# Splitting minus the score maxima before the transpose: bf16 products, a dense copy, and one 512-column addition per head

## What is computed

```python
scores = jnp.einsum('bhqd,bhkd->bhqk', q, k) / np.sqrt(D_HEAD)      # window, cells, masked
scores = jnp.where(local[None, None, :, :], scores, -jnp.inf)       # windowed attention only
attn = jax.nn.softmax(scores, axis=-1)
ctx = jnp.einsum('bhqk,bhkd->bhqd', attn, v)
```

## Time and profile before

| | |
|---|---|
| median of 3 runs | 3567.08 us (3566.13 to 3568.82) |
| the profiled execution | 3568.07 us, of which the span is 3566.3 us |
| PE busy | 3242.3 us, 91% of the span |
| DVE, ACT, POOL busy | 65%, 48%, 29% |
| granted TensorE clock, mean | 0.964 of full speed |
| stores of the 16 results | first at 510.4 us, last at 3563.7 us |

### The profile page before, as it was taken

The page is one execution under the profiler, slowest core; times in us unless marked ns, Lnnn a source line. Parts: engine busy times, 40 slices in busy tenths (PEclk is TensorE's granted clock), DMA queues, the critical chain, the costliest instruction groups (busy, mean ns, idle before and its releaser), DMA issues.

```text
span 3566.3 us, 77500 instructions
## 1 busy us (share of the span) xinstructions
PE 3242.3 (91%) x31372; PEld 2395.2 (67%) x31372; DVE 2329.9 (65%) x4137; ACT 1695.1 (48%) x3472; POOL 1019.1 (29%) x795
## 2 busy tenths in 40 slices
PE   7899999998999999899999999999899999999876
PEld 6777767676766667676666766667676666766644
DVE  6675658667676766767577675766767676464533
ACT  1244454544545455444635445354454545554532
POOL 7872006042331413333041332304233141000000
PEclk8999999999999999999999999999999999999986
DMA  6210011010101101010100101101010110100000
GB/s 207 89 45 31 19 29 39 29 40 19 46 19 40 31 23 46 16 41 26 37 28 25 43 19 37 31 29 39 19 46 19 40 31 16 37 14 10 13 7 4
DMA packets 123276, 122.88 MB, mean 34 GB/s; under 512 B 9776, under 2 KB 122672, under 8 KB 122800
## 3 DMA queue, kind: packets, MB, share of 16 engines
q1 hardware_dynamic: 122928, 117.91, 10.9%
HBM read 113.69 MB, written 4.19 MB: 33 GB/s over the span
## 4 chain that ended last, share of the span: by engine, by line
PE 60%; DVE 15%; ACT 9%; issue 8%; POOL 7%; DMA 1%; SPq 0%; DVEq 0%; POOLq 0%; ACTq 0%
PE banks L747 16%; PE banks L739 11%; PE banks L892 7%; PE banks L917 6%; DVE nmx L1251 5%; PE banks L945 5%; POOL work L1641 3%; ACT work L1482 3%; PE banks L732 2%; PE banks L754 2%; PE banks L855 2%; PE banks L903 2%; POOL work L1631 2%; PE banks L952 1%; PE banks L921 1%
## 5 line engine op out<-in xcount | busy, mean ns | idle before, releaser
L747 PE MATMUL banks<-work,weights 128*128 128x256 f32 x3584 | 868.3, 390 | 56.4 <-DVE work L1275 51.5
L1251 DVE TENSOR_REDUCE nmx<-banks 128x4 f32<-128x1024 f32 (+3 forms) x684 | 725.4, 1099 | 250.5 <-PE banks L892 248.7
L747 PEld LDWEIGHTS banks<-work,weights 128*128 128x128 f32 x3584 | 678.3, 194 | 189.0 <-DVE work L1275 53.9
L1482 ACT ACTIVATE work<-banks 128x1024 f32<-128x1024 f32 (+3 forms) x679 | 595.1, 937 | 288.7 <-PE banks L921 288.7
L739 PE MATMUL banks<-weights,work 128*128 128x256 f32 x2688 | 653.7, 389 | 20.7 <-ACT work L1482 4.4
L739 PEld LDWEIGHTS banks<-weights,work 128*128 128x128 f32 x2688 | 499.3, 193 | 124.9 <-issue 39.7
L1641 POOL TENSOR_TENSOR work<-work 128x512 f32<-128x512 f32 x256 | 407.3, 1615 | 366.4 <-DVE work L1221 216.9
L892 PE MATMUL banks<-work 32*128 32x256 f32 (+1 forms) x5120 | 357.5, 394 | 60.5 <-DVE nmx L1251 27.2
L917 PE MATMUL banks<-work 32*128 32x256 f32 (+1 forms) x5120 | 391.4, 394 | 18.0 <-DVE nmx L1251 6.8
L1631 POOL TENSOR_TENSOR work<-work 128x512 f32<-128x512 f32 x256 | 346.6, 1375 | 148.7 <-DVE work L1217 134.7
L1269 DVE TENSOR_TENSOR added<-work 128x1024 f32<-128x1024 f32 x192 | 281.3, 1469 | 129.3 <-ACT work L1482 118.7
(11 more groups left out here) (156 smaller groups left out, 3525.2 us busy)
## 6 DMA issues: line engine op xcount, KB each, us to landing
weights<-in_w_all SPq DMA_DIRECT2D x322, 256.0 KB, 2.8
work<-in_w_setup SPq DMA_DIRECT2D x41, 256.0 KB, 5.1
work<-in_ctx SPq DMA_DIRECT2D x32, 256.0 KB, 3.1
work<-in_x SPq DMA_DIRECT2D x16, 256.0 KB, 3.0
out<-work SPq DMA_DIRECT2D x16, 256.0 KB, 2.2
weights<-in_w_all SPq DMA_DIRECT2D x1, 3072.0 KB, 15.0
row<-in_rows SPq DMA_DIRECT2D x1, 1280.0 KB, 9.2
mrow<-in_mask SPq DMA_DIRECT2D x16, 32.0 KB, 3.2
```

Of the source, the lines that this page charges most:

```text
L747: ins = e.matmul(b[:, m * 256:m * 256 + 256], wslot(w)[:, k, m * P:m * P + P], xin[:, k, :], start=(k == 0 and (m == 0 or closed)) if star ...
L1251: ins = e.tensor_reduce(nmax(s, n)[:, 2 * p + j:2 * p + end, :], b.rearrange("p j (c n) -> p j c n", c=NC)[:, :, :, 0:w], AX, ALU.max, neg ...
L1482: ins = e.activation(dst, b.rearrange("p j (c n) -> p j c n", c=NC)[:, :, :, 0:w], ACT.Exp)
```

## The change

Three edits. The two transposes per head group become two products of the bf16 view of `nmx` (its upper halves, which hold all three parts) with a bf16 identity. The copy behind them writes bf16, so the three rows lie densely in the first half of the slot. And for cells and masked heads the addition comes after both key chunks, as one product of 512 columns per head (the rows read twice by a stride of 0) in place of two of 256; only the first chunk's product then clears the bank. Windowed heads keep two additions per head. In the plan `nm` costs 0.16 in place of 0.22, and the seed list is another.

```diff
-SEEDS = (981929, 264616, 376881, 660340, 622402, 125658, 701981, 998496, 712956, 113630)
+SEEDS = (404952, 898653, 559752, 353328, 253142)
...
-        b = do("PE", "nm", n, 0.22, *maxed, *((st_done[n - 2],) if n >= 2 else ()), takes=("misc",))
+        b = do("PE", "nm", n, 0.16, *maxed, *((st_done[n - 2],) if n >= 2 else ()), takes=("misc",))
...
-        def upper(t):
-
-            return t.bitcast(BF16).rearrange("p (n h) -> p n h", h=2)[:, :, 1]
+        def nmax_parts(s, n, c):
+
+            return small[s]["nmx"].bitcast(BF16)[:, n % 2, c].rearrange("p (n h) -> p n h", h=2)[:, :, 1]
...
-            return slot(s, NMT[quad(n)[0]])[:, n % 2, :]
+            return slot(s, NMT[quad(n)[0]])[:, n % 2, :].bitcast(BF16)[:, 0:S]
...
-                        ins = e.transpose(b[:, c * P:c * P + P], small[s]["nmx"][:, a % 2, c, :], ident[:, :])
+                        ins = e.matmul(b[:, c * P:c * P + P], nmax_parts(s, a, c), ident_bf[:, :], start=True, stop=True)
...
-                                     q[32 * g:32 * g + 32, f, qq], start=(kind != "x"), stop=False,
+                                     q[32 * g:32 * g + 32, f, qq], start=(kind != "x" and kc == 0), stop=False,
                                      tile_position=(32 * g, 0))
...
+                    if kind != "x":
                         for g in range(4):
-                            ins = e.matmul(b[g // 2][g % 2][:, o], ones_bf[32 * g:32 * g + 3, :],
-                                           upper(stored_nmax(s, a))[32 * g:32 * g + 3, qq], start=False,
-                                           stop=(kind != "x" or kc == NC - 1), tile_position=(32 * g, 0))
-                            if kc == NC - 1 and g == 1:
+                            ins = e.matmul(b[g // 2][g % 2].rearrange("p (c n) -> p c n", c=NC), ones_bf[32 * g:32 * g + 3, :],
+                                           stored_nmax(s, a)[32 * g:32 * g + 3, :].unsqueeze(1).broadcast_to([3, NC, S]),
+                                           start=False, stop=True, tile_position=(32 * g, 0))
+                            if g == 1:
                                 ins.then_inc(*tell(pe[s], "st mm", a, 0, i))
```

More of the change, by code:

```diff
@@ L917, in tensor @@
                             e.matmul(b[g // 2][g % 2][:, o], k[32 * g:32 * g + 32, f, kc * P:kc * P + P],
[L918 removed]
+                                     q[32 * g:32 * g + 32, f, qq], start=(kind != "x" and kc == 0), stop=False,
                                      tile_position=(32 * g, 0))
+                        if kind == "x":
+                            for g in range(4):
+                                ins = e.matmul(b[g // 2][g % 2][:, o], ones_bf[32 * g:32 * g + 3, :],
+                                               stored_nmax(s, a)[32 * g:32 * g + 3, qq], start=False,
+                                               stop=(kc == NC - 1), tile_position=(32 * g, 0))
+                                if kc == NC - 1 and g == 1:
+                                    ins.then_inc(*tell(pe[s], "st mm", a, 0, i))
+                    if kind != "x":
                         for g in range(4):
[L921 to L924 removed]
+                            ins = e.matmul(b[g // 2][g % 2].rearrange("p (c n) -> p c n", c=NC), ones_bf[32 * g:32 * g + 3, :],
+                                           stored_nmax(s, a)[32 * g:32 * g + 3, :].unsqueeze(1).broadcast_to([3, NC, S]),
+                                           start=False, stop=True, tile_position=(32 * g, 0))
+                            if g == 1:
                                 ins.then_inc(*tell(pe[s], "st mm", a, 0, i))
```

## The result

The changed kernel takes 3528.19 us (median; 3522.43 to 3536.69) where the kernel before, on the same chip, takes 3566.61. The ratio is 0.9896, with a 95% interval of 0.9869 to 0.9923: faster by 1.0%, some 38 us. The profiled execution took 3533.58 us, with a span of 3531.8 and a mean granted clock of 0.965 (0.964 before). The other three took 3522.43, 3522.80 and 3536.69, the two short ones at 0.968, so the profile shows one of the two longer ones.

What follows compares the result with a forecast made beforehand. TensorE (PE), busy 3242.3 of 3566.3 us, was taken as the bound. 1.3 + 0.3 + 1.0 + 0.5 + 1.8 - 1.0 = 3.9 us per cycle, 43 over eleven, plus 8 at start and end, gave 3516; full range 3460 to 3562.

Steps and rivals of the forecast that it cites:

- Work: Shorter `nm` and additions on PE: 14 x 0.09 = 1.3 us plus 16 x 0.02 = 0.3 us less per cycle.
- The rival that the weight load of 103 ns paces the slot: At `nm`: the slot still costs 0.22 us and the order gives nothing; 5 us at most, 3563; chance 0.08.
- Place B: PE's 4.3 us wait of `co` for `norm`: one sum and one wait go, 1.0 us less per cycle.
- Place C: Masked stretch, `y_q_t` to `y_o`: 0.5 us of `y_q_t`'s wait and 1.8 of other waits less per cycle.
- Place A: Three `s` ahead of `down`, where `nm` waits for the `split`: 1.0 us more per cycle.
- slower rival: At place A splits come late, PE waits over 3 us and the clock falls: 3600; chance 0.10.
- The clock: `co` at half clock behind its wait: 2.25 us would go at full clock, but none counted.
- What I said would make the forecast wrong: `nm` keeping 0.2, stores over 210 us apart, or a half-clock stretch vanishing or appearing, each worth 2 us per cycle.
- The start: Start and end: 8 us less from the work; the new order there counted as 0, with 10 either way.
- the collapse of waits: All laid-out gains come and the clock stays up: 9.5 us per cycle, 3454, or 3489 with two thirds; chance 0.17.
- work alone: Waits sum to 15.9 us per cycle as before, merely elsewhere; only shorter work counts: 3541; chance 0.20.

Runs made afterwards that it cites:

- e11: Changed kernel's new order with only the one addition of 512 columns; old float32 transposes and copy: 3542.83 us, 0.9940 of the kernel before.
- e5: Kernel before plus 14 products that add zero, ahead of the first `co` cell's wait in every entry: 3565.73 us, 1.0006 of the kernel before.
- e6: The three edits in the old order, plus 14 products that add zero ahead of the first `co` cell's wait: 3541.15 us, 0.9953 of the kernel before.
- e2: Kernel before with the new seed list and planned cost, so the new order with the old work: 3550.67 us, 0.9955 of the kernel before.
- e1: Changed kernel's three edits with the old seed list and planned cost, so the old order: 3561.43 us, 0.9997 of the kernel before.
- e9: Changed kernel's work, with the old order for steps planned before 700 us and the new order after: 3499.48 us, 0.9814 of the kernel before.
- e12: Changed kernel with the old order up to 700 us, plus 11 zero products ahead of the first `co` cell's wait: 3497.29 us, 0.9809 of the kernel before.
- e3: Old order with the bf16 transposes and dense copy, but two additions of 256 columns per head: 3560.23 us, 0.9991 of the kernel before.

## Why the prediction came out right, and where its steps were off

The forecast of 3516 lies 12 us below the median and the range holds the result, but that the number came so near is luck: two larger errors met. The ten cycles gave 68.7 us where the sum had 43 for eleven, and start and end together cost 34 where the sum had a gain of 8.

**Work.** `nm` slot forecast 0.13, measured 0.11 in the place that the earlier trace rows shows; additions 0.24 to 0.22 forecast, no change in the cycle measured (e11). The 0.22 of before was read in one place and taken for all: ahead of other steps the slot was 0.27 to 0.37, and the gain is 0.11 to 0.15. The forecast of 1.6 us per cycle for both was measured at 1.2 (e5 against e6) and 1.0 to 1.2 (e2 against after), though the slot was better than forecast: PE's busy time fell by 1.8 (193.71 to 191.89), and the rest of that went into waits, so fewer than the 14 `nm` that I counted are on the path; which ones was not tried. For start and end I forecast 8; e1 has 5.5 and 3.4. By the Trainium skill (TensorE: Matmul & The Clock Gate, "Back-to-back issue gap") with its 81 ns per product and weight load at 128 columns the slot would have been 0.16 by an estimate. The trace has 0.055 to 0.067 from one product's start to the other's, and decides against it for a pair ahead of a dense step; a long stream of such pairs, of which the page speaks, is in no run here. The rival that the weight load of 103 ns paces the slot fell with the same row: the loads take 99 ns on average, and the second product starts 0.055 us behind the first.

**Place B.** Forecast 1.0 less, `co` to wait 3 to 3.5; measured 4.29 to 3.33. Right in size, but only in part for the reason given: from the start of the layer norm's L1191 to `co` it was 3.97 us (1650.73 to 1654.70) and is 3.44 (1658.62 to 1662.06), mostly because this instruction took 2.13 us in place of 2.58. Over half of the 0.96 us is that, and not the sum that went.

**Place C.** The waits laid out, 3.6 less, of which I took half, plus 0.5 for `y_q_t`, 2.3 in all. `y_q_t` still waited 0.56 of 0.63, so that term fell. But the layout of 35.3 us for the stretch was nearly exact: measured 35.0, and PE's waits in it fell by 1.85 us, from 5.04 to 3.19, where I took 1.8. The other 1.15 us are busy time, although there is 0.85 us more of work inside: the stretch at half clock is gone, and the `nm` are shorter.

**Place A.** Forecast 1.0 more. Measured: waits of 1.82 + 0 + 0.15 against 1.81, so 0.2 more. The first `nm` waits what it did, not 0.7, and the two behind it next to nothing, since `down` of 3.7 us stands between. The mechanism of the slower rival was there in a small form: the clock falls behind this wait in one cycle of three.

**The clock, the step that failed.** "A wait of over 3 us is left, so I count none" was the largest miss within the cycle. The stretch behind `co` went from 6.8 to 3.4 us though the wait still passed 3, and the masked one vanished: PE's work at half clock went from 7.9 to 4.4 us per cycle, worth 1.8 us. The rest of the fall of 6.85 us is 1.7 of busy time (the edits) and 3.4 of waits, for which I forecast 1.6 and 2.3: B 0.96, C 1.85, A 0.16 more in place of 1.0 more, and 0.7 elsewhere. This division is read from the timelines; no run changed place B or C alone. What I said would make the forecast wrong, a stretch at half clock that vanishes, took place, and the stores are 204.75 apart and not 207 to 208. The price that I gave, 2 us for each, was too high: e5 and e6 have 1.1 to 1.5.

**The start, the other miss.** "The order there is another too, for which I have no reading: 0, with 10 either way." It was 33.5 us (e2), far out of that bound. I could have laid out the masked stretch of the first entry like that of place C; whether that would have found the loss was not tried. e9 shows that the loss belongs to the order of the first two entries: with the old start the same kernel takes 3499.

So of the rivals, the collapse of waits was nearest in the cycle (with two thirds of it at 6.3) and its 3489 is within 11 us of what e9 and e12 reached with the old start; work alone is refuted as the cause (e1 at 0.9997), although its 3541 lies only 13 us above the result.

## What to carry to other kernels

Test the edits in the old order and the new order without the edits before believing either: here the edits alone gave nothing, the order alone 0.45%, both 1.0%; in the old order the saved time of each cycle came back as waits and a stretch at half clock. Where a planner's numbers change the order, read start, cycle and end apart, from the stores, and choose the order of each by itself: the old start with the new cycle was worth nearly as much again as the whole change (0.9814 against 0.9896). Price a wait of PE by its length and by what runs behind it: a stretch of 3.4 us of work at half clock costs this cycle 1.1 to 1.5 us, one in which PE stands still costs less, and one wait shortened may hand the fall to another. Price a short step in more than one place: the same two transposes held 0.22 to 0.37 us, by what came next.

## What the runs showed that I had not expected

- Less work, same cycle: with 2 us less of PE's work per cycle, e1 and e3 kept 211.6 to 211.8 in all cycles, with 13.6 us at half clock in place of 10.2.
- Nearly the same wait at place A, 1.82 or 1.83 us, is followed by the half clock in one cycle of three (after). In e1 (1.93 us) it is in each, and in before (1.81) in none.
- A pair of bf16 products of 128 columns, each with its own weight load of 99 ns, takes 0.111 us ahead of the band's step, and the float32 transposes took 0.218. Ahead of the scores of `st` it is 0.205 and 0.31.
- Four additions of 3 rows and 512 columns take as long as eight of 256: the slot of a group's `st` stayed at 1.27 to 1.29 us. That the columns pace them and not their number is the plain reading, which no run isolates.
